# Packing the pair products by way of a DRAM scratch, in ten contraction steps where there were eleven

## The reference

```python
e = jnp.stack([tbl_0[ids[:, 0]], ..., tbl_49[ids[:, 49]]], axis=1)      # (2048, 50, 16)
gram = jnp.einsum('bid,bjd->bij', e, e)
z = gram[:, I_IDX, J_IDX]                                              # pairs i < j: 1225
h = jnp.concatenate([z, dense_ctx], axis=1)                            # 1241
h = jnp.maximum(h @ W_top1 + b_top1, 0.0)                              # 512
h = jnp.maximum(h @ W_top2 + b_top2, 0.0)                              # 256
y = h @ W_top3                                                         # 1
```

## Time and profile before

| | |
|---|---|
| runs | 452.11, 452.78, 453.46 us |
| profiled execution, its own time | 453.39 us |
| its span (first to last instruction) | 451.3 us |
| mean granted clock of PE | 0.890 of full speed |
| busy: PE, DVE, ACT, POOL | 342.9, 295.8, 198.8, 322.7 us |
| DMA from SP's and ACT's queues | 35.04 MB |

### The profile page before, as it was taken

One profiled execution on the slowest core, in us unless ns is written; L12 is line 12 of the kernel. 1 busy time (PEld: TensorE's weight loads), 2 busy tenths in 40 slices (PEclk: granted clock), 3 DMA queues, 4 the chain that ended last, 5 costly groups with the idle time before them and its releaser, 6 DMA issues.

```text
span 451.3 us, 13158 instructions
## 1 busy us (share of the span) xinstructions
PE 342.9 (76%) x5633; PEld 247.4 (55%) x5633; DVE 295.8 (66%) x606; ACT 198.8 (44%) x288; POOL 322.7 (71%) x318
## 2 busy tenths in 40 slices
PE   0568167566488979979989699798895948989886
PEld 0567067565366657666666476656653525454543
DVE  2599899999357579758576687566715437165551
ACT  2335712246235774455457653445487324140511
POOL 5788777777777777787777777778777777776020
PEclk9978659978679997989999969699998895988999
DMA  6994503423321344243213433111121222212020
GB/s 161 407 367 142 173 7 101 118 77 86 82 44 39 104 115 94 63 136 88 47 32 103 115 95 65 36 43 36 40 53 24 66 50 50 48 15 61 5 61 1
DMA packets 24638, 38.92 MB, mean 86 GB/s; under 512 B 8532, under 2 KB 15876, under 8 KB 24452
## 3 DMA queue, kind: packets, MB, share of 16 engines
q1 hardware_dynamic: 14166, 35.04, 24.0%
q0 software_dynamic: 9920, 2.55, 6.6%
q10 hardware_dynamic: 494, 0.49, 0.3%
HBM read 26.98 MB, written 0.14 MB: 60 GB/s over the span
## 4 chain that ended last, share of the span: by engine, by line
PE 34%; DVE 18%; ACT 13%; SPq 11%; issue 10%; DMA 8%; POOL 5%; another core or an unknown queue 0%; DVEq 0%; ACTq 0%; POOLq 0%
PE hid_ps L881 12%; SPq L383 11%; DVE onehot L490 9%; PE look_ps L803 8%; ACT gram L1010 6%; POOL emb L448 5%; DMA ids_bc<-ids_dram 5%; PE mid_ps L938 5%; PE gram_ps L820 3%; ACT z_both L1077 2%; DVE turned L604 2%; PE gram_ps L841 2%; ACT looked L1047 2%; DMA z_both<-gram 2%; DVE w_sb L672 1%
## 5 line engine op out<-in xcount | busy, mean ns | idle before, releaser
L448 POOL DMA_INDIRECT emb<-tbl,gidx x304 | 318.9, 1049 | 95.7 <-issue 88.4
L881 PE MATMUL hid_ps<-w_sb,z_both 127*128 127x512 f16 x462 | 112.3, 386 | 0.0
L803 PE MATMUL look_ps<-parts,onehot 125*128 125x64 f16 x1836 | 75.0, 203 | 44.5 <-DVE onehot L490 29.9
L490 DVE TENSOR_SCALAR onehot<-ids_bc,rows 125x2048 f16<-125x2048 f16 (+1 forms) x144 | 92.2, 690 | 19.2 <-PE look_ps L803 14.7
L803 PEld LDWEIGHTS look_ps<-parts,onehot 125*128 125x128 f16 x1836 | 69.5, 105 | 56.2 <-issue 20.8
L1010 ACT ACTIVATE gram<-gram_ps 50x784 f32<-50x784 f32 x96 | 78.2, 815 | 29.6 <-PE gram_ps L820 26.7
L803 PE MATMUL look_ps<-parts_med,onehot 125*128 125x128 f16 x800 | 57.1, 233 | 14.4 <-DVE onehot L490 13.8
L881 PEld LDWEIGHTS hid_ps<-w_sb,z_both 127*128 127x128 f16 x462 | 41.5, 99 | 46.1 <-issue 3.3
L803 PEld LDWEIGHTS look_ps<-parts_med,onehot 125*128 125x128 f16 x800 | 53.1, 105 | 20.6 <-DVE parts_med L663 13.9
L490 DVE TENSOR_SCALAR onehot<-ids_bc,rows_med 125x1024 f16<-125x1024 f16 x100 | 45.8, 495 | 28.2 <-PE look_ps L803 24.4
L1047 ACT ACTIVATE looked<-look_ps 128x1024 f16<-128x1024 f32 (+1 forms) x28 | 26.7, 954 | 67.0 <-PE look_ps L803 66.6
(11 more groups left out here) (74 smaller groups left out, 221.7 us busy)
## 6 DMA issues: line engine op xcount, KB each, us to landing
ids_bc<-ids_dram SPq DMA_DIRECT2D x28, 512.0 KB
emb<-tbl,gidx POOLq DMA_INDIRECT x304
z_both<-gram SPq DMA_DIRECT2D x31, 121.0 KB
z_both<-w SPq DMA_DIRECT2D x1, 2816.0 KB
z_both<-gram SPq DMA_DIRECT2D x31, 90.8 KB
z_both<-gram SPq DMA_DIRECT2D x152, 6.2 KB
z_both<-gram SPq DMA_DIRECT2D x31, 60.5 KB
gram<-small SPq DMA_DIRECT2D x2, 512.0 KB, 5.1
```

The source lines that it names most:

```text
L448: pool.indirect_dma_start(emb[:, T % TPC, f, :], None, big[f], bass.IndirectOffsetOnAxis(ap=gidx[:, T, f:f + 1], axis=0)).then_inc(landed, 16)
L490: nc.vector.tensor_scalar(onehot[0:TP, s % RING, 0:cnt, :], ids_bc[0:TP, o % IDS_BUFS, 0:cnt, :], row, None, ALU.is_equal).then_inc(onehot ...
L803: last = nc.tensor.matmul(bank[:, half, at:at + width], onehot[0:TP, at_ring, i, t * TILE:(t + 1) * TILE], moving.rearrange("p i s d -> p ...
L881: return nc.tensor.matmul(hid_ps[:, :], z_parts[0:KP, T % 2, x, k, :], w1_sb[0:KP, k, w, :], start=(i == 0), stop=(i == L1_MM - 1))
```

## The change

`gram` keeps all 50 columns. Each side of a tile (50 partitions x 3200 floats, 640,000 bytes) is stored whole to a DRAM scratch `gram_dram`. Then four DMAs read the pairs back. In the scratch, row p starts at element 50 p, and the reads step by `SKEW` = 51 from an offset of 1: partition p gets 25 consecutive columns from its diagonal on, wrapping into the next row. Because the matrix is symmetric, 49 rows x 25 columns hold each of the 1225 pairs once. The 25 columns are laid out as 10 + 10 + 5, on partitions 0 to 48, 49 to 97 and 98 to 122 (the last five columns as two pieces), so the contraction has 125 partitions x 10 steps: 30 matmuls a tile instead of 33. Both sides go in one DMA; together the four pieces move 627,200 bytes.

SP now waits for the evacuation, stores, waits for `z_split`, loads the dense numbers, waits for the store to land (`saved`), and issues the four reads. `gram` is free once `saved` has arrived. For the last tile SP stores side 0 and reads pieces 0 and 1, ACT stores side 1 and reads pieces 2 and 3, and POOL issues nothing.

```diff
-ST = 11
...
+ST = 10
+RUN = NF // 2
+SKEW = NF + 1
+PIECES = [(0, NF - 1, 0, ST, 0, 0), (0, NF - 1, ST, ST, NF - 1, 0),
+          (0, RUN, 2 * ST, RUN - 2 * ST, 2 * (NF - 1), 0), (RUN, NF - 1 - RUN, 2 * ST, RUN - 2 * ST, 2 * (NF - 1), ST // 2)]
-LAST_KS = (range(0, 6), range(6, ST))
+LAST_KS = (range(0, ST // 2), range(ST // 2, ST))
+        gram_dram = nc.dram_tensor("gram_dram", (2, TWO, NF * NF * COLS), F32).ap()
-        gram = sb("gram", [128, 2, NCOL * COLS], F32)
+        gram = sb("gram", [128, 2, NF * COLS], F32)
+        def saving(T, a):
+            return (gram_dram[T % 2, a, :].rearrange("(r n) -> r n", r=NF),
+                    gram[a * STEP:a * STEP + NF, T % 2, :])
-        def piece_of(piece, T, a):
+        def piece_of(piece, T):
             r0, nr, c0, ncol, p0, k0 = piece
...
+            runs = gram_dram[T % 2, :, COLS:].rearrange("a (p q b) -> p a q b", q=SKEW, b=COLS)
+            return (z[p0:p0 + nr, T % 2, :, k0:k0 + ncol, :].rearrange("p a k b -> p a (k b)"),
+                    runs[r0:r0 + nr, :, c0:c0 + ncol, :].rearrange("p a q b -> p a (q b)"))
             def pack(T, sides=range(TWO), pieces=PIECES):
...
                 if T < FINAL:
                     sp.wait_ge(gram_copied, TWO * EVACS * (T + 1))
                 else:
                     sp.wait_ge(half_by_act, halves_of(T))
-                    sp.wait_ge(half_by_dve, halves_of(T))
+                    if T < LAST:
+                        sp.wait_ge(half_by_dve, halves_of(T))
+                sp.wait_ge(packed[T % 2], PIECE_INC * (T // 2))
                 for a in sides:
-                    for piece in pieces:
-                        out, src = piece_of(piece, T, a)
-                        sp.dma_start(out, src).then_inc(packed[T % 2], 16)
+                    out, src = saving(T, a)
+                    sp.dma_start(out, src).then_inc(saved[T % 2], 16)
...
+                sp.wait_ge(saved[T % 2], SAVE_INC * (T // 2 + 1))
+                for piece in pieces:
+                    out, src = piece_of(piece, T)
+                    sp.dma_start(out, src).then_inc(packed[T % 2], 16)
-            pack(NTILES - 1, (0,), BIG_PIECES)
+            pack(LAST, (0,), PIECES[:2])
...
-                    act.wait_ge(packed[T % 2], PIECE_INC * (T // 2))
+                    act.wait_ge(saved[T % 2], SAVE_INC * (T // 2))
...
-            def pack(T, pieces):
+            def pack(T):
+                act.wait_ge(half_by_dve, halves_of(T))
+                act.wait_ge(packed[T % 2], PIECE_INC * (T // 2))
+                out, src = saving(T, 1)
+                act.dma_start(out, src).then_inc(saved[T % 2], 16)
                 act.wait_ge(z_split, T - 1)
-                act.wait_ge(half_by_act, halves_of(T))
-                act.wait_ge(half_by_dve, halves_of(T))
-                for piece in pieces:
-                    out, src = piece_of(piece, T, 1)
+                act.wait_ge(saved[T % 2], SAVE_INC * (T // 2 + 1))
+                for piece in PIECES[2:]:
+                    out, src = piece_of(piece, T)
                     act.dma_start(out, src).then_inc(packed[T % 2], 16)
```

More of the change, by code:

```diff
@@ L72 @@
 MED_HALF = MED_SIZE // PRM // 2
-ST = 11
[L77 to L87, removed]
+ST = 10
[3 more added lines that the diff above has]
+          (0, RUN, 2 * ST, RUN - 2 * ST, 2 * (NF - 1), 0), (RUN, NF - 1 - RUN, 2 * ST, RUN - 2 * ST, 2 * (NF - 1), ST // 2)]
+TOP = RUN - 2 * ST
+DENSE_P = 2 * (NF - 1) + RUN
 DENSE_R = 2
@@ L90 @@
 KP = DENSE_P + DENSE_R
-NCOL = NF - 1
 HID1, HID2 = 512, 256
@@ L291, in build @@
         packed = [sem(f"packed{h}") for h in range(2)]
+        saved = [sem(f"saved{h}") for h in range(2)]
         packs_begun = sem("packs_begun")
@@ L330, in evacuation @@
                 .rearrange("p j (k b) -> p j k b", k=Q)
-            return out, src[:, a, 0:NCOL]
+            return out, src[:, a]
         def half_evacuation(T, h, a):
@@ L366, in pack @@
             def pack(T, sides=range(TWO), pieces=PIECES):
+                if T < FINAL:
+                    sp.wait_ge(gram_copied, TWO * EVACS * (T + 1))
+                else:
+                    sp.wait_ge(half_by_act, halves_of(T))
+                    if T < LAST:
+                        sp.wait_ge(half_by_dve, halves_of(T))
+                sp.wait_ge(packed[T % 2], PIECE_INC * (T // 2))
+                for a in sides:
+                    out, src = saving(T, a)
+                    sp.dma_start(out, src).then_inc(saved[T % 2], 16)
                 if T >= 2:
@@ L464, in _ @@
                 gathers(T)
-            pool.wait_ge(z_split, LAST - 1)
-            pool.wait_ge(half_by_act, halves_of(LAST))
-            pool.wait_ge(half_by_dve, halves_of(LAST))
-            for a in range(TWO):
-                for piece in CORNERS:
-                    out, src = piece_of(piece, LAST, a)
-                    pool.dma_start(out, src).then_inc(corners_in, 16)
         @block.vector
@@ L1188, in _ @@
                 copy_half(LAST, h)
-            pack(LAST, BIG_PIECES)
+            pack(LAST)
             for i in range(len(LAST_KS)):
@@ L1207, in pair_rows @@
             for k in range(ncol):
-                if c0 + k < r0 + r:
-                    i, j = sorted((FIELD[c0 + k], FIELD[r0 + r]))
-                    at[p0 + r, k0 + k] = i * (2 * NF - i - 1) // 2 + j - i - 1
-                    seen += 1
+                i, j = sorted(FIELD[f] for f in divmod((r0 + r) * SKEW + 1 + c0 + k, NF))
+                at[p0 + r, k0 + k] = i * (2 * NF - i - 1) // 2 + j - i - 1
+                seen += 1
+    assert len(set(at.flat)) == NF * (NF - 1) // 2 + 1
     assert seen == NF * (NF - 1) // 2
```

19 lines of the change are left out of this document (5 added, 14 removed).

## The result

The changed kernel takes 469.47 us (median of four runs, 467.97 to 472.11) against 453.12 us for the kernel before: a ratio of 1.036, 95% interval 1.0292 to 1.0428, slower by 16 us. The forecast was 458.0 us with a range to 462.0. The direction was right, the size wrong.

A forecast was written before the change was run, and what follows sets the result against it. The prediction took POOL's gathers as the bound, with only the tail deciding: PE starts the last first layer at 440.3, plus 6.6, 2.7 for the clock and 6.9 gives a 456.5 span, 458.0 us on the median's footing; range 451.0 to 462.0.

The forecast's parts named there:

- The steady part costs nothing: Tiles before the tail: savings and longer packs lie beside the gathers; 0 us, with -1.5 to +1.5.
- about 13 us: Steady tiles, from evacuated to packed: no longer than the 13.4 us of issue and a landing before.
- The new traffic doesn't slow the gathers: Steady part: 1.28 MB stored and 0.63 MB read a tile leave gathers unslowed; one took the usual 0.94 us at 448 GB/s.
- PE's rest in the tail gains 1.3 us: Tail from 379.6 us: fewer matmuls let tile 15's dot products start at 419.6, evacuated at 427.2 instead of 428.52.
- The last pack, 12.3 us: Last tile, evacuated to packed: store 7.1 us, then reads 5.0, plus wakes; before 6.97 us, bounds 7.9 to 15.2.
- The fixed 1.7 us: Last tile's pack: fixed part of a transfer's landing, counted once for the stores and once for the reads.
- the rate of 232 KB/us: Last tile's store: rate taken from a 116 KB store and a 232 KB load; 1250 KB in 1.7 + 5.4 us.
- The rule of the Trainium skill: Last tile's transfers: 50 rows over 10 engines, 49 over 7, 25 over 5; round trip 11.4 us, sum 457.1.
- The clock: Last first layer: after 5.1 us of PE idling, half speed for the first 5.5 us, 2.7 us more.
- half way: Rival, last tile: round trip about 10 us, clock holds through 2.8 us of idling, 453.0 us, no change; chance 0.15.
- Sum: Whole kernel: 440.3 + 6.6 + 2.7 = 449.6, then 6.9 us to the end: span 456.5, time 458.0.
- the steady part turns: Rival, last ten tiles: ACT waits longer, dot products slip, POOL waits for PE; 5 us more, 463; chance 0.05.

The follow-up runs named there:

- e5_steady: The changed kernel with the stores of its last four tiles (12 to 15) left out, their reads taking older tiles' data: 457.15 us, 1.0108 of the kernel before.
- e6_tail: The changed kernel with stores for tiles 0, 1 and 12 to 15 only: 467.02 us, 1.0283 of the kernel before.
- e9_ten: The kernel before with 30 of its 33 matmuls a tile, the eleventh step's pairs left out of the result: 453.57 us, 0.9992 of the kernel before.
- e7_dram16: The changed kernel storing only 16 of the 50 columns to DRAM from tile 2 on: 454.90 us, 1.0011 of the kernel before.
- e15_thirds48: The changed kernel with stores in three column pieces and reads cut 48 + 1, 16 + 9 and 16 + 8 rows: 461.30 us, 1.0137 of the kernel before.
- e2_both48: The changed kernel with stores cut 48 + 2 rows and reads 48 + 1, 16 + 9, 16 + 8: 463.27 us, 1.0209 of the kernel before.
- e3_nostore: The changed kernel storing tiles 0 and 1 only, later tiles reading what those left: 453.20 us, 0.9956 of the kernel before.

## Why the prediction was wrong

- **The steady part costs nothing: the step that failed first.** POOL did not slow, as forecast. But the round trip was not "about 13 us": from store to ACT's pass it took 16.1 us at tile 10, the store alone 9.7 to 11.1. The forecast held it against the pack before and said that ACT's waits "stay or shrink"; they went from 11.1 to 41.2 us, and ACT's evacuations, PE's dot products and the next store stand behind them in order. PE entered the tail 11.4 us late, more than the 5.2 us that it used to idle there. That leaves 3.2 us at tile 15's dot products, and `e5_steady`, which has only the steady part's stores, has the same 3 us (423.90 for 424.21).
- **The new traffic doesn't slow the gathers: wrong too, but hidden here.** I read it from POOL's issue alone, which indeed stays (mean 1.04 us, before 1.05). What the traffic delays is the landing: 2.26 us from start to use was taken as fixed and became 7.7 us. In the profiled execution of the changed kernel PE came to those rows 1.6 and 2.7 us after they were turned, so this costs it nothing that the round trip had not cost already. It would show as soon as the steady part were mended: in `e6_tail` PE idled 6.61 us for the rows.
- **PE's rest in the tail gains 1.3 us, tile 15 evacuated at 427.2:** measured 437.7. Its dot products began 4.6 us behind the forecast. The other 5.9 us are the wait for tile 14's pack, for which the forecast had no term: PE's stall of 2.54 us and the half clock after it. The gain itself is not resolved by `e9_ten`.
- **The last pack, 12.3 us:** measured 14.7, within the bounds of 7.9 to 15.2. The store was mis-sized: 8.9 us for 7.1. The fixed 1.7 us holds (1.8 by `e7_dram16`), the rate of 232 KB/us does not: 175. A rate from the difference of two transfers half a microsecond apart, one of them a load, was too thin. The reads took 5.8 for 5.0.
- **The rule of the Trainium skill** ("DMA: Bandwidth & Descriptors", section "Why a DMA increments its semaphore by 16 and not by 1"): the shares agree with it. By it 50 rows go over 10 of 16 engines, which is 0.62, measured 0.64; 49 rows go over 7, which is 0.44, measured 0.47; with 48 rows the store's share rose to 0.81 and 0.87. The time of the store does not follow: it landed no sooner at the larger share, so an estimate of its rate from the number of engines fails here. For the reads the gain is 0.7 us in the last tile (5.8 to 5.1), and it comes once a tile, as the 5 us of `e15_thirds48` suggest.
- **The clock: right.** PE idled 5.64 us, the layer began at 1.2 GHz, and its 30 matmuls took 453.17 to 462.02, 8.9 us, where 9.3 was forecast. Not foreseen: the earlier stall of 2.54 us at 425 took the clock down as well, from 427 to 440. That speaks against the rival *half way*, which had the clock hold through 2.8 us.
- **Sum.** Of the 12.4 us between the forecast span and the measured one, 4.6 were there at tile 15's dot products, 5.9 came up to its evacuation and 2.4 in the last pack; the rest gives 0.5 back. Of the rivals, "the steady part turns" named the first of these (ACT waiting longer for packs, dot products slipping), but at 0.05, and sought its sign in POOL's waits, which did not grow: the slip used up PE's idle time, not POOL's.

## What to carry to other kernels

When a pack is made longer, ask first which engine's in-order work stands behind its wait: here ACT's evacuations did, and through them PE's dot products and the next store, so that a longer trip came round again with every tile. When a transfer of a megabyte is added, look also at when other transfers land (from issue to the first instruction that uses the data), not only at how long their issue takes: a queue can issue undisturbed while its data come 5 us late. And before a late landing is called the cause, look whether the engine that needs the data idled for it; two delays that end at nearly the same time hide each other, and taking one away shows the other. A round trip by way of a store pays fixed costs twice and one half must land before the other starts. And a store's rate is to be measured at its own size: spreading it over more engines can raise their busy share and leave the landing where it was.

## What the hardware did that was not expected

- 1250 KB stored from 2 x 50 partitions landed in 8.9 us at a DMA share of 0.64 and in 8.8 us at 0.81 to 0.87 (`e2_both48`); 400 KB took 4.1 us to DRAM and 4.9 to SBUF.
- Rows gathered 1.0 to 6.1 us behind such a store were used 0.1 to 1.1 us after it landed, in thirteen cases; in `e6_tail`, where no store is ahead of tiles 10 to 12, 2.4 us after their last gather. Reads from the scratch alone made it 4.7 us once (`e3_nostore`).
- Cutting the store into runs of 2,560 bytes lengthened the last one from 8.9 to 10.2 us.
